# Unread products in TensorE's standstills, and the first two quarter units issued by groups, in a resnorm-GNN-LSTM kernel

## The reference, cut to what matters

```python
x = _layernorm(x + _L0_gnn_ref(x, adj, ...), axis=-1)
x = _layernorm(x + _L1_gnn_ref(x, adj, ...), axis=-1)

# _L0: agg = A_hat @ features; h = relu(batchnorm(agg @ W1.T + b1)); out = batchnorm(h @ W2.T + b2)
# _L1:
h = jax.nn.relu(jnp.einsum('ts,bsh->bth', adj, x @ Wg0 + bg0))
h = jax.nn.relu(jnp.einsum('ts,bsh->bth', adj, h @ Wg1 + bg1))
for p in range(1, MAX_SKIP + 1):          # MAX_SKIP = 4
    nw = Tv // p
    wins = h[:, :nw * p, :].reshape(Bv * nw, p, Hd)
    last = _lstm_last(Wih[p - 1], Whh[p - 1], bih[p - 1], bhh[p - 1], wins)
    idx = jnp.arange(nw) * p + (p - 1)
    h = h.at[:, idx, :].set(last.reshape(Bv, nw, Hd))
```

## Time and profile before

| | |
|---|---|
| median of 3 runs | 766.74 us (766.21 to 769.2) |
| the profiled execution, its own time | 765.86 us |
| its span, first to last instruction | 763.8 us |
| TensorE busy | 731.7 us, 96% of the span |
| VectorE / ScalarE / GpSimd busy | 86% / 70% / 42% |
| mean granted TensorE clock | 0.984 |

### The profile page before, as it was taken

How to read it: one execution, slowest core, us unless ns; L and a number is a source line. 1 busy time by engine, 2 the same in 40 slices (tenths; PEclk the granted TensorE clock), 3 DMA queues, 4 the chain that set the end, 5 groups by cost and what they waited for, 6 DMA issues and landing times.

```text
span 763.8 us, 11248 instructions
## 1 busy us (share of the span) xinstructions
PE 731.7 (96%) x3890; PEld 416.8 (55%) x3890; DVE 659.8 (86%) x1399; ACT 533.4 (70%) x856; POOL 323.3 (42%) x292
## 2 busy tenths in 40 slices
PE   7999899789999999998999999999999999999994
PEld 5777444467776777763444444444444444554542
DVE  5888687889989899857998789889999898899987
ACT  3778888537776877748887786687676757666662
POOL 1000000078888878820000000800990946239986
PEclk9999899989999999999999999999999999999998
DMA  5553300014243242312500000100011021011012
GB/s 152 168 151 97 111 0 2 0 56 111 56 111 87 80 111 56 84 29 100 231 1 1 0 1 1 42 1 1 2 42 42 13 99 42 1 70 57 15 55 83
DMA packets 64604, 45.04 MB, mean 59 GB/s; under 512 B 1658, under 2 KB 63524, under 8 KB 63524
## 3 DMA queue, kind: packets, MB, share of 16 engines
q1 hardware_dynamic: 64548, 44.33, 18.9%
HBM read 27.55 MB, written 16.78 MB: 58 GB/s over the span
## 4 chain that ended last, share of the span: by engine, by line
PE 72%; DVE 17%; ACT 7%; issue 3%; POOL 0%; DMA 0%; POOLq 0%; DVEq 0%
PE ps L643 10%; PE ps L644 10%; PE ps L652 10%; PE ps L613 8%; PE ps L648 7%; PE ps L657 7%; PE ps L649 7%; PE ps L561 4%; ACT work L848 4%; DVE ln_stats L1086 3%; DVE ring L1068 2%; DVE ring L1104 2%; DVE store L1115 2%; PE ps L572 2%; PE ps L573 2%
## 5 line engine op out<-in xcount | busy, mean ns | idle before, releaser
L848 ACT ACTIVATE work<-ps,gate_bias 128x512 f32<-128x512 f32 x449 | 282.6, 680 | 91.7 <-PE ps L657 57.8
L643 PE MATMUL ps<-store,wih 128*128 128x512 f16 x449 | 169.0, 376 | 3.5 <-issue 2.3
L644 PE MATMUL ps<-store,wih 128*128 128x512 f16 x449 | 168.9, 376 | 0.0
L652 PE MATMUL ps<-store,wih 128*128 128x512 f16 x449 | 158.0, 376 | 0.0
L530 POOL TENSOR_TENSOR end_mv<-end_mv,minus_half 128x12 f32<-128x12 f32 (+1 forms) x16 | 31.0, 1940 | 257.2 <-DVE end_mv L1080 257.2
L521 POOL TENSOR_SCALAR ring<-ring,ln_mv 128x128 f32<-128x128 f32 x120 | 120.6, 1017 | 2.7 <-POOL ln_mv L511 2.5
L1051 DVE TENSOR_TENSOR work<-work 128x512 f32<-128x512 f32 (+1 forms) x129 | 88.2, 684 | 22.6 <-ACT work L855 22.6
L855 ACT ACTIVATE work<-store 128x512 f32<-128x512 f32 x97 | 60.5, 623 | 52.9 <-DVE store L1044 36.3
L648 PE MATMUL ps<-store,whh 128*128 128x512 f16 (+1 forms) x248 | 93.2, 376 | 0.0
L649 PE MATMUL ps<-store,whh 128*128 128x512 f16 (+1 forms) x248 | 93.1, 376 | 0.0
L657 PE MATMUL ps<-store,whh 128*128 128x512 f16 (+1 forms) x248 | 93.0, 376 | 0.0
(11 more groups left out here) (126 smaller groups left out, 1254.8 us busy)
## 6 DMA issues: line engine op xcount, KB each, us to landing
ring<-in_x_dram SPq DMA_DIRECT2D x32, 256.0 KB, 2.9
ring<-in_x_dram SPq DMA_DIRECT2D x16, 512.0 KB, 5.3
x_scratch<-ring SPq DMA_DIRECT2D x16, 512.0 KB, 3.5
ring<-x_scratch SPq DMA_DIRECT2D x5, 1024.0 KB, 4.8
out_dram<-ring SPq DMA_DIRECT2D x5, 768.0 KB, 3.6
store<-x_scratch SPq DMA_DIRECT2D x3, 1024.0 KB, 14.1
out_dram<-store SPq DMA_DIRECT2D x3, 768.0 KB, 4.1
out_dram<-ring SPq DMA_DIRECT2D x5, 256.0 KB, 2.3
```

The lines of the kernel that those rows point to most:

```text
L643: nc.tensor.matmul(acc(j), w_hi, x_hi, start=True, stop=False)
L644: nc.tensor.matmul(acc(j), w_lo, x_hi, start=False, stop=False)
L652: last = nc.tensor.matmul(acc(j), weights(wih, j)[0], x_lo, start=False, stop=u.first)
L848: nc.scalar.activation(acts[:, n % 2, gate, 0:u.cols], ps[:, gate_bank(q), 0:u.cols], ACT.Tanh if gate == G else ACT.Sigmoid, bias=gate_bi ...
```

## The change

TensorE gets a helper, `keep_busy(bank, times)`, that multiplies the constant `ones` by itself into a PSUM bank that nobody reads at that moment, each time one single-precision product of 128 columns. It is called at ten places up to the first group, 54 products in all. In front of the run of 15 a wait for `chan_stored` at 62 is added, which protects the bank. The second part replaces `lstm_unit` for units 28 and 29 by `blocked_group`: each of these units is issued in two halves of 256 columns, first the half of group 14 for both units, then the half of group 15 for both.

```diff
+            def keep_busy(bank, times):
+                for _ in range(times):
+                    nc.tensor.matmul(ps[:, bank, 0:P], ones[:], ones[:], start=True, stop=True)
+
+            pe.wait_ge(consts_done, N_CONSTS - 2)
+            keep_busy(3, 3)
             pe.wait_ge(consts_done, N_CONSTS)
             pe.wait_ge(ld_adj, 16)
             nc.tensor.transpose(ps[:, 0, 0:P], adj_n[:], ident[:]).then_inc(prep_pe, 1)
+            keep_busy(3, 2)
             pe.wait_ge(ld_w12, 32)
...
             last.then_inc(prep_pe, 1)
+            keep_busy(3, 3)
             pe.wait_ge(prep_dve, SCALED_STEP)
...
+            keep_busy(3, 1)
             pe.wait_ge(prep_dve, AHAT_STEP)
             aggregate(0)
...
             for job in range(W_FIRST):
                 turn_weights(job)
+            pe.wait_ge(chan_stored, H1 * (CHUNKS - 1))
+            keep_busy(OUT[0], 15)
...
             for job in range(W_FIRST, W_JOBS):
                 turn_weights(job)
+            keep_busy(H0[0], 12)
...
+            def blocked_group(n, g):
+                u = UNITS[n]
+                def gate(j):
+                    return gate_columns(ps[:, gate_bank(GATE0[n] + j), :], u)[:, g, :, :]
+                def weights(j, part):
+                    return wih[:, part, u.gates[j] * P:(u.gates[j] + 1) * P]
+                hi, lo = (unit_input(u, part)[:, g, :, :] for part in range(2))
+                pe.wait_ge(gnn_hi_done, 2 * (N_BLOCKED_GROUP + g + 1))
+                for j in range(len(u.gates)):
+                    wait(pe, gate_done, gate_before(GATE0[n] + j) + 1)
+                    nc.tensor.matmul(gate(j), weights(j, 0), hi, start=True, stop=False)
+                    nc.tensor.matmul(gate(j), weights(j, 1), hi, start=False, stop=False)
+                pe.wait_ge(gnn_lo_done, 2 * (N_BLOCKED_GROUP + g + 1))
+                for j in range(len(u.gates)):
+                    last = nc.tensor.matmul(gate(j), weights(j, 0), lo, start=False, stop=True)
+                    if g == 1:
+                        last.then_inc(gate_summed, 1)
+
-            def turn_z(g):
+            def turn_z(g, busy=(0, 0)):
...
                     last.then_inc(z_turned, 1)
+                    keep_busy(H0[0], busy[h])
...
                     last.then_inc(u0_summed, 1)
+                    if g == 0 and h == 0:
+                        keep_busy(H0[0], 4)
...
-            turn_z(0)
-            turn_z(1)
+            turn_z(0, busy=(0, 2))
+            turn_z(1, busy=(6, 6))
...
             pe.wait_ge(u1_copied, 2 * GROUPS)
-            for n in range(N_GROUPED, N_EARLY):
+            for n in (N_GROUPED, N_GROUPED + 1):
+                blocked_group(n, 0)
+            for n in (N_GROUPED, N_GROUPED + 1):
+                blocked_group(n, 1)
+            for n in range(N_GROUPED + 2, N_EARLY):
                 lstm_unit(n)
```

More of the change, by code:

```diff
@@ L312, in resnorm_gnn_kernel @@
         TURN = 6
+        N_BLOCKED_GROUP = GROUPS - 2
         ld_adj, ld_w12, ld_wg, ld_vec, ld_bg = (
```

## The result

| | before | after |
|---|---|---|
| median | 766.48 us (4 runs, 766.09 to 769.2) | 760.44 us (4 runs, 760.35 to 760.65) |
| ratio | | 0.9914, 95% interval 0.9891 to 0.9937 |
| span of the profiled execution | 763.8 us | 758.9 us |
| mean granted clock | 0.984 | 0.995 |

The change makes the kernel 6.0 us faster by the medians; 761.4 was forecast, with 759.8 to 764.6 as the range. The profiled spans differ by 4.9 us only: of the 1.1 us between the two figures 0.3 is time outside the span (765.86 - 763.8 = 2.06 us before, 760.65 - 758.9 = 1.75 after), the rest is the distance of the profiled executions from their medians. The executions of before are spread over 3.1 us, those of after over 0.3. The experiments point to falls of the clock that the profile of before does not show.

A forecast was written before the change was run, and what follows sets the result against it. TensorE, busy 96% of the span, was taken as the bound, so gains come from its standstills or half-clock stretches. -1.6 - 2.6 - 0.35 - 0.7 = -5.25 takes 765.86 to 760.6, median 761.4 us, range 759.8 to 764.6.

The forecast's parts named there:

- Opening: Kernel start to `aggregate(2)`: unread products bring TensorE's clock up by 9.06 us; -1.6 us, bounds 0 and -1.8.
- First batch norm: Wait before the second layer: fifteen unread products fit and keep the clock full; -2.6 us, bounds 0 and -2.74.
- Second batch norm: Up to group 1: clock kept full, but VectorE and GpSimd's scaling limit the gain; -0.35 us, bounds 0 and -0.39.
- Quarter units: Units 28 and 29, end of grouped stage: half products let ScalarE's first gate start earlier; -0.7 us, bounds -0.9 and +2.0.
- The sum: All four terms, -5.25 us: profiled execution 765.86 to 760.6, with its distance from the median carried over, 761.4.
- Rival 1: Low-clock stretches shorter in the median run than in the profiled one: sum -3.2, median 763.5; 0.28 together with rival 2.
- Rival 2: Only part of the unread products hold the clock, opening gains 0: sum -3.65, 763.1 us; 0.28 together with rival 1.
- Rival 3: Unread products do not count for the clock, which falls as before: slower, 769.5 us, up to +5.5; chance 0.07.
- Rival 4: The change does nothing, gains being taken up by the grouped stage with VectorE's rhythm: 766.7 us; chance 0.05.

The follow-up runs named there:

- E2: The kernel before plus only the 9 unread products of the opening, quarter units whole; median 764.33 us, ratio 0.9982.
- E6: The changed kernel without the 30 unread products from the second batch norm to group 1; median 762.6 us, ratio 0.9951.
- E7: The changed kernel with 30 unread products for 15 in the first batch norm; median 762.98 us, ratio 0.9961.
- E9: The changed kernel with 5 unread products for 15 in the first batch norm; median 761.86 us, ratio 0.9943.
- E10: The changed kernel with all unread products but the quarter units issued whole, as before; median 762.22 us, ratio 0.9947.
- E5: The changed kernel with thirty 128-column transposes for the fifteen unread products in the first batch norm; median 760.65 us, ratio 0.9929.
- E11: The changed kernel with whole quarter units and 9 unread products in the 2.33 us standstill ahead of them; median 760.94 us, ratio 0.9934.
- E1: The kernel before plus only the quarter units by groups, no unread product; median 764.95 us, ratio 0.9989.
- E3: The kernel before plus only the 15 unread products in the first batch norm and their wait; median 766.39 us, ratio 0.9995.
- E8: The changed kernel with the turning of the small vectors moved behind the first chunk's channel products; median 759.44 us, ratio 0.9914.
- E4: The kernel before plus only the 30 unread products from the second batch norm to group 1; median 763.91 us, ratio 0.9976.

## Why the prediction was right, point by point

**Opening, -1.6 forecast, 1.34 measured in the profile.** The mechanism held: the clock was up before 9.06. L565 came at 6.48 (6.35 worked out), hidden behind the vectors as said. The term was mis-sized because I took the landing of the last vector DMA for a fixed anchor at 9.06. It was 9.50 in this execution, and 9.50 - 9.06 = 0.44 is what is missing: from this anchor to `aggregate(2)` it takes 12.08 - 9.50 = 2.58 us for 4.36, a gain of 1.78. In others it was 8.87 to 9.63, with `aggregate(2)` at 11.44 to 12.21 (E2, E6, E7, E9 and E10). In two the products did not bring the clock up so early: `aggregate(0)` still took 1.82 us in E5 and 1.70 in E11, and `aggregate(2)` stands at 12.29 and 12.56.

**First batch norm, -2.6 forecast, 2.57 measured.** Also the products' length: 84.43 - 80.92 = 3.51 with the overlapping end, for 3.35.

**Second batch norm, -0.35 forecast, 0.19 measured,** within its bounds, for the reason given: VectorE without a pause, then GpSimd. But the sentence "So ten microseconds of low clock are worth at most 0.39" holds for the profiled execution only. E6 puts the 30 products at 2.2 us by medians (762.6 - 760.44), and its profile, at 3.2, breaks the premise: there VectorE did wait for TensorE.

**Quarter units, -0.7 forecast, 0.85 measured.** A half product costs 0.109 us, 0.11 was taken. TensorE was free 2.19 us behind the start of `mix_gnn`, a little earlier than I had put it, which is the difference. The second effect, that the units fill a standstill in which the clock can fall, was not in the text; by E10 and E11 it is the larger one by medians, 1.3 us of 1.8.

**The sum** was -5.25 for the profiled execution. Its span moved by 4.9 and the four terms add up to 4.95; that the time of the profiled executions moved by 5.21 (765.86 to 760.65) is 0.3 us of luck outside the span. **The step that failed** is the last: "That execution is 0.9 us below the median of the runs shown, 766.74, which I carry over". (By its own terms it gives 761.5 and not 761.4.) The forecast of the median was 1.0 too high because the changed kernel has no slower median to carry over to: its median is 760.44, its profiled execution 760.65. The executions of before that took longer than the profiled one seem to have lost the difference in ways that this profile does not show and that the change removed as well. In the runs of before that stand beside the experiments, time goes with the mean granted clock:

| mean granted clock, before | executions | us |
|---|---|---|
| 0.985 to 0.987 | 36 | 763.5 to 765.6 |
| 0.982 to 0.983 | 15 | 766.0 to 767.6 |
| 0.980 | 16 | 767.0 to 769.9 |

From 0.987 to 0.980 is some 10 us more of low clock, as an estimate (0.007 of 764 us, twice, since the low level is half). The profiled execution, 0.984 and 765.86 us, lies between the groups, and over half of these executions were faster than it. Where the clock fell in the executions above 766 us is not known, because only one execution of before has a profile. Two more places are candidates, since in kernels with the same code there the clock fell: the wait inside group 0 (E1, E3 and E6) and the 2.33 us one ahead of the quarter units (E2 and E3). A low stretch at the second batch norm that lies badly, as in E6, is a third. The profile after has a full clock at all three, as have those of E5 and E8, and the executions after lie within 0.3 us.

**Rival 1** was right in its mechanism and did not decide the sum. The low stretch does vary: the first eight instructions of the second layer took 6.17 us before, 5.24 in E1, 5.15 in E2 and 5.28 in E4, for 3.60 at the full clock, so its removal is worth 1.6 to 2.6 us, and the profile of before was the dearest of the four. The rule of the Trainium skill ("TensorE: Matmul & The Clock Gate", Part 1: The HAM clock gate) that the point of release varies from run to run agrees: in these four kernels, with the same code at this place, the clock came back 5.3 us behind the layer's first product before, and 4.0, 3.3 and 4.6 us behind it in E1, E2 and E4. But the number of falls varies too, and that went the other way. **Rival 2** did not occur in the profile after: the products of the opening held. E5 and E11 show a mild form of it. **Rival 3** did not occur; the unread products count: the granted clock is 1.00 from 82 to 92 us. **Rival 4** did not occur: the grouped stage passed every shift on. What stays open is why the first batch norm alone (E3) had so poor a median, 1.8 us above that of before beside it; its profile shows a fall at both other places, and whether the shift of 2.6 us makes these falls more frequent was not tried.

## What to carry to other kernels

A standstill of TensorE of two or three microseconds can cost a second time behind it, through the clock, and whether it does changes from execution to execution. One profile shows only the falls that happened in it; take the mean clock of many executions beside their times, and a second profile where they differ. Measure the kernel before beside each version, since its median moved by 2.4 us here. Fill each such wait with work that ends just before the wait does: with too little the clock fell here (E9), and too much is paid nearly in full (E7). Real work moved into the wait is better than unread products by what it saves itself.

## What the runs showed of the hardware that I had not expected

- Thirty single-precision transposes of 128 columns in 3.44 us held the clock through the wait as fifteen products did (E5). The Trainium skill, "TensorE: Matmul & The Clock Gate", Part 4: PE-mode transpose, says that the full clock does not engage for transposes; here, with the clock already full, it stayed, though with the 16 turned blocks ahead TensorE did nothing but transposes from 79.38 to 84.57 us. No run tries a long row of transposes from the low clock.
- In group 0 the clock fell at waits of 1.89, 1.92 and 2.13 us (E1, E3, E6) and not at 1.72 and 1.65 (before, E2). But the wait of 2.33 us ahead of whole quarter units brought a fall in E2 and E3 and none in before, E4 and E10. The length of the wait alone does not decide.
- Many falls came when TensorE was at work again: 0.2 us after the wait in E3 (162.9), 0.5 and 1.1 at the same place in E1 and E6, 1.3 in E9 (85.4). A clock that is full when work resumes is not yet safe.
- Products of a constant with itself hold the clock as products of data do: it is 1.00 through the fifteen products and behind them, from 82 to 92 us.
